# The fourth head of the last attention pass by token halves, and a half of x2 in another tile

## The reference, cut to what matters

```python
attn = softmax(einsum('bthd,bshd->bhts', q, k) * scale)          # 16 heads of 128
attn_out = einsum('bhts,bshd->bthd', attn, v) @ out_w + out_b
x = x + gate1 * attn_out
x2 = _ln(x) * (1.0 + scale2) + shift2
h = gelu(x2 @ ffn_w1 + ffn_b1)
x = x + gate2 * (h @ ffn_w2 + ffn_b2)
```

## Time and profile before

| what | before |
|---|---|
| median of 3 runs | 482.5 us (482.31 to 483.1) |
| the profiled execution: its time | 482.44 us |
| its span on the core | 480.6 us |
| TensorE's granted clock, mean | 0.999 |
| busy in the span: PE / DVE / ACT / POOL | 467.4 / 389.3 / 318.9 / 48.0 us |

### The profile page before, as it was taken

How to read it: one execution, slowest core, us unless ns; L and a number is a source line. 1 busy time by engine, 2 the same in 40 slices (tenths; PEclk the granted TensorE clock), 3 DMA queues, 4 the chain that set the end, 5 groups by cost and what they waited for, 6 DMA issues and landing times.

```text
span 480.6 us, 13808 instructions
## 1 busy us (share of the span) xinstructions
PE 467.4 (97%) x5271; PEld 334.8 (70%) x5271; DVE 389.3 (81%) x1368; ACT 318.9 (66%) x950; POOL 48.0 (10%) x78
## 2 busy tenths in 40 slices
PE   7999999999999999999899999999999999999997
PEld 4455776557656676568545444788898988989886
DVE  4969895779768899997896997888888888888884
ACT  1677964788477966887476965565665656656563
POOL 3010240223020320223000000000000000000000
PEclk9999999999999999999999999999999999999999
DMA  8992510100201000000000000000000000000000
GB/s 283 419 388 70 135 45 22 62 25 23 66 22 44 22 0 2 0 2 1 1 1 1 0 1 0 3 3 1 0 1 11 12 0 12 0 12 11 1 12 23
DMA packets 10399, 20.85 MB, mean 43 GB/s; under 512 B 1472, under 2 KB 4992, under 8 KB 9728
## 3 DMA queue, kind: packets, MB, share of 16 engines
q1 hardware_dynamic: 9808, 19.89, 12.0%
q10 hardware_dynamic: 560, 0.60, 0.4%
HBM read 19.40 MB, written 1.08 MB: 43 GB/s over the span
## 4 chain that ended last, share of the span: by engine, by line
PE 88%; DVE 4%; ACT 3%; DMA 1%; issue 1%; POOL 1%; SPq 0%; DVEq 0%
PE bank L884 58%; PE score L884 27%; PE spare L884 2%; DMA ao_sb<-xtok 1%; POOL ptx L507 1%; ACT ptx L632 1%; ACT ao_sb L585 1%; DVE drive L1459 1%; ACT x L532 0%; ACT th L810 0%; DVE drive L1463 0%; DVE q_group L2112 0%; DVE tok_stats L1406 0%; DVE acc L1551 0%; DVE drive L1614 0%
## 5 line engine op out<-in xcount | busy, mean ns | idle before, releaser
L884 PE MATMUL bank<-x,pairs_store 128*128 128x512 f16 x384 | 86.3, 379 | 0.5 <-ACT x L532 0.4
L884 PEld LDWEIGHTS bank<-x,pairs_store 128*128 128x128 f16 x384 | 36.9, 98 | 43.4 <-issue 1.4
L507 POOL TENSOR_TENSOR ptx<-pt,ptx 32x256 f16<-32x256 f32 x62 | 43.2, 697 | 176.2 <-ACT ptx L632 172.8
L884 PE MATMUL score<-cub,neg_eye 128*128 128x64 f32 x256 | 55.6, 299 | 0.0
L585 ACT ACTIVATE big<-bank,head_b 128x512 f16<-128x512 f32 x60 | 39.8, 685 | 17.4 <-PE bank L884 17.0
L2026 DVE TENSOR_TENSOR thlo<-th 128x64 f16<-128x64 f32 x128 | 28.8, 225 | 26.0 <-ACT th L811 24.8
L884 PE MATMUL score<-th,coup_part 128*128 128x32 f16 x1024 | 46.2, 177 | 0.9
L884 PE MATMUL bank<-pairs_store,ao_sb 128*128 128x256 f16 x360 | 43.0, 273 | 0.7 <-issue 0.2
L884 PE MATMUL bank<-pairs_store,x 128*128 128x512 f16 x192 | 43.4, 379 | 0.0
L810 ACT ACTIVATE th<-score 128x64 f16<-128x64 f32 x96 | 21.5, 224 | 31.7 <-PE score L884 28.9
L884 PEld LDWEIGHTS bank<-pairs_store,ao_sb 128*128 128x128 f16 x360 | 34.0, 98 | 7.5 <-DVE ao_sb L1652 1.5
(11 more groups left out here) (252 smaller groups left out, 1052.1 us busy)
## 6 DMA issues: line engine op xcount, KB each, us to landing
wqk_sb<-wqk SPq DMA_DIRECT2D x16, 256.0 KB, 2.7
wv_sb<-wv SPq DMA_DIRECT2D x4, 512.0 KB, 5.4
wo_sb<-wo SPq DMA_DIRECT2D x4, 512.0 KB, 4.2
f_sb<-ffn_w SPq DMA_DIRECT2D x2, 1024.0 KB, 14.7
ao_sb<-xtok SPq DMA_DIRECT2D x4, 256.0 KB, 5.8
x_sb<-xT SPq DMA_DIRECT2D x1, 1024.0 KB, 12.5
w_sb<-w1T SPq DMA_DIRECT2D x1, 1024.0 KB, 16.1
w_sb<-w2T SPq DMA_DIRECT2D x1, 1024.0 KB, 16.9
```

The lines of the kernel that those rows point to most:

```text
L507: nc.gpsimd.tensor_tensor(ptx[s, 1, :, s], pt[s], ptx[s, 0, :, s], ALU.subtract).then_inc(ptx_ready, 1)
L884: return nc.tensor.matmul(dst, lhsT, rhs, start=start, stop=stop, **kw)
```

## The change

In the last pass, the fourth head's work after the scores is cut into two token halves. DVE and ACT copy, shift, exponentiate, normalise and place half 0, then half 1, and `mix_half` forms the values' products of one half at a time. On PE, `out_project(0, 3, [0, 1])` and `mix_half(3, 1)` stand behind the output products of quarters 0 and 1, and those of quarters 2 and 3 for the last two heads stand behind `turn_normed(0)`, in the place of eight `unread` matmuls. `ada_late(SHIFT2)` moves forward into `spare`. On DVE, `low_last_pv([1])` stands between the layer norm's statistics and its root, and `take_heads(2)` and `take_heads(3)` stand one place later. ACT's `empty_x2(0)` follows `x1_high(NH)`. The modulated first half of x2 is written to `centred`, since `drive` still holds the gates of quarters 2 and 3. The first layer's blocks get the uses 163, 164, 162, 165, 166, 168, 169, 167 in the place of 162, 165, 166, 163, 164, 167, 168, 169. Lines that are only "..." mark what is left out.

```diff
...
-USE_F1 = [[AFTER + n for n in (2, 5, 6, 3, 4, 7, 8, 9)], [AFTER + 3 * KB + MB + m for m in range(MB)]]
+USE_F1 = [[AFTER + n for n in (3, 4, 2, 5, 6, 8, 9, 7)], [AFTER + 3 * KB + MB + m for m in range(MB)]]
...
+            if i == NQUAD - 1 and j == QUAD - 1:
+                for h in range(NH):
+                    gs = slice(h * G // 2, (h + 1) * G // 2)
+                    pool.wait_ge(full[bank_of(LAST_PV[j - 1] + h)], i * NPAR + count_of(LAST_PV[j - 1] + h))
+                    for q in range(NB4 // 2):
+                        s = slice(q * T, (q + 1) * T)
+                        pool.wait_ge(high_placed, i * (QUAD * NB4) + NB4 * (j + h) + q + 1)
+                        nc.gpsimd.tensor_tensor(ptx[s, 1, gs, s], pt[s, gs], ptx[s, 0, gs, s], ALU.subtract
+                                                ).then_inc(half_placed[h], 1)
+                return
             if j == QUAD - 1:
-                use = (LAST_PV if i == NQUAD - 1 else USE_PV)[j - 1] + 1
+                use = USE_PV[j - 1] + 1
...
-            for q in range(NB4 // 2 if i == NQUAD - 1 and j == QUAD - 1 else NB4):
+            for q in range(NB4):
...
-    pool.wait_ge(ptx_ready, NQUAD * QUAD * NB4)
+    for h in range(NH):
+        pool.wait_ge(half_placed[h], NB4)
...
-            nc.scalar.activation(x1_pair[:, 0, k, s], drive[:, k, s], ACT.Copy).then_inc(x1_high_ready, 1)
+            src = centred[:, k] if n == NH else drive[:, k, s]
+            nc.scalar.activation(x1_pair[:, 0, k, s], src, ACT.Copy).then_inc(x1_high_ready, 1)
...
+        def copy_half(h):
+            act.wait_ge(scores_ready, NQUAD * QUAD + h)
+            for q in range(NB4 // 2):
+                s, gs = slice(q * T, (q + 1) * T), slice(h * G // 2, (h + 1) * G // 2)
+                nc.scalar.activation(sraw[s, gs], s8[s, gs, s], ACT.Copy).then_inc(half_copied[h], 1)
...
+        def exps_half(h):
+            gs = slice(h * G // 2, (h + 1) * G // 2)
+            act.wait_ge(shifted, NQUAD * QUAD + h)
+            nc.scalar.activation(pe_[:, gs], sc[:, gs], ACT.Exp, scale=SCALE / WSCALE ** 2).then_inc(exp_ready, 1)
...
+        def place_high_half(h):
+            use = LAST_PV[QUAD - 2] + h
+            act.wait_ge(full[bank_of(use)], i * NPAR + count_of(use))
+            act.wait_ge(pt_ready, NQUAD * QUAD + h)
+            for q in range(NB4):
+                s, gs = slice(q * T, (q + 1) * T), slice(h * G // 2, (h + 1) * G // 2)
+                nc.scalar.activation(ptx[s, 0, gs, s], pt[s, gs], ACT.Copy).then_inc(high_placed, 1)
...
-        copy_scores(3, NB4 // 2 if last else NB4)
-        place_high(2)
-        exps(3)
-        if not last:
+        if last:
+            copy_half(0)
+            copy_half(1)
+            place_high(2)
+            exps_half(0)
+            exps_half(1)
+            place_high_half(0)
+            empty_pv(2)
+            empty_pv(3, [0])
+            place_high_half(1)
+            mlp_highs(5, 7)
+            empty_pv(3, [1])
+            mlp_highs(7, 8)
+        else:
+            copy_scores(3)
+            place_high(2)
+            exps(3)
...
-        empty_pv(2, [0])
-        place_high(3)
-        empty_pv(2, [1])
-        if last:
-            mlp_highs(5, 7)
-        else:
+            empty_pv(2, [0])
+            place_high(3)
+            empty_pv(2, [1])
...
-        empty_pv(3)
-        if last:
-            mlp_highs(7, 8)
-        else:
+            empty_pv(3)
...
+    act.wait_ge(first_heads_out, 1)
...
+    x1_high(NH)
+    act.wait_ge(last_full, 1)
...
-    x1_high(NH)
...
-                last = parts3(score[:, g // 4, (g % 4) * P:(g % 4 + 1) * P], q, k)
-            last.then_inc(scores_ready, 1)
+                done = parts3(score[:, g // 4, (g % 4) * P:(g % 4 + 1) * P], q, k)
+                if g == G - 1 or last and j == QUAD - 1 and g == G // 2 - 1:
+                    done.then_inc(scores_ready, 1)
...
+        def mix_half(j, h):
+            base = i * (QUAD * NB4) + NB4 * (j + 1)
+            late = j == QUAD - 1
+            pe.wait_ge(high_placed, base + NB4 * h if late else base)
+            dst = score[:, h] if late else fill(use_pv[j] + h)
+            for g in range(4 * h, 4 * h + 4):
+                at = dst[:, (g % 4) * P:(g % 4 + 1) * P]
+                for part in range(2):
+                    mm(at, v_sb[:, g, part, j * DH:(j + 1) * DH], ptx[:, 0, g], g % 4 == 0 and part == 0, False,
+                       skip_group_check=True)
+            if late:
+                pe.wait_ge(half_placed[h], NB4)
+            else:
+                pe.wait_ge(ptx_ready, base)
+            for g in range(4 * h, 4 * h + 4):
+                done = mm(dst[:, (g % 4) * P:(g % 4 + 1) * P], v_sb[:, g, 0, j * DH:(j + 1) * DH], ptx[:, 1, g],
+                          False, g % 4 == 3, skip_group_check=True)
+            if late:
+                done.then_inc(pv_full, 1)
+            else:
+                done.then_inc(full[bank_of(use_pv[j] + h)], 2)
...
                     if first:
-                        pe.wait_ge(ada2_ready, 4)
+                        pe.wait_ge(ada2_ready, 5)
...
+            elif last and (pair, c) == (0, 3):
+                done.then_inc(first_heads_out, 1)
...
+        if last:
+            mix_half(2, 0)
+            mix_half(2, 1)
+            out_project(0, 2, [0, 1])
+            mix_half(3, 0)
+            out_project(1, 0, [2])
+            out_project(1, 1, [2])
+            pe.wait_ge(ada2_ready, 4)
+            ada_late(SHIFT2, spare)
+            out_project(1, 0, [3])
+            out_project(1, 1, [3])
+            mix_half(3, 1)
+            out_project(0, 3, [0, 1])
+            return out_project
...
-    attention_pass(NQUAD - 1, True)
+    out_project = attention_pass(NQUAD - 1, True)
...
-    ada_late(SHIFT2, fill(USE_F1[0][3]))
-    unread(score[:, 0], 3)
+    pe.wait_ge(pv_taken, NQUAD * NH)
+    unread(score[:, 0], 4)
...
-    unread(fill(USE_F1[0][4])[:], 8)
+    for c in (2, 3):
+        out_project(1, c, [2, 3])
...
-    pe.wait_ge(ada2_ready, 5)
...
+    def modulated(h, k):
+        return drive[:, k, HALF:N] if h else centred[:, k]
...
-        s = slice(h * HALF, (h + 1) * HALF)
...
-        V.tensor_tensor(tok(drive[:, k, s]), tok(score[:, k]), mod(SCALE2, k, h), ALU.mult).then_inc(turned_read, 1)
+        V.tensor_tensor(tok(modulated(h, k)), tok(score[:, k]), mod(SCALE2, k, h), ALU.mult).then_inc(turned_read, 1)
...
-        s = slice(h * HALF, (h + 1) * HALF)
...
-        V.tensor_tensor(tok(drive[:, k, s]), tok(drive[:, k, s]), mod(SHIFT2, k, h), ALU.add).then_inc(normed, 1)
+        V.tensor_tensor(tok(modulated(h, k)), tok(modulated(h, k)), mod(SHIFT2, k, h), ALU.add).then_inc(normed, 1)
...
-        V.tensor_tensor(x1_pair[:, 1, k, s], drive[:, k, s], x1_pair[:, 0, k, s], ALU.subtract).then_inc(x1_low_ready, 1)
+        V.tensor_tensor(x1_pair[:, 1, k, s], modulated(h, k), x1_pair[:, 0, k, s], ALU.subtract).then_inc(x1_low_ready, 1)
...
+        def half_strips(h):
+            gs = halves_of(h)
+            dve.wait_ge(scores_ready, NQUAD * QUAD + h)
+            for q in range(NB4 // 2, NB4):
+                s = slice(q * T, (q + 1) * T)
+                V.tensor_copy(sraw[s, gs], s8[s, gs, s]).then_inc(half_copied[h], 1)
...
+        def shift_half(h):
+            gs = halves_of(h)
+            dve.wait_ge(half_copied[h], NB4)
+            own.step(V.tensor_reduce(smax[:, gs], sraw[:, gs], AX_X, ALU.max))
+            own.wait()
+            V.tensor_tensor(sc[:, gs], sraw[:, gs], smax[:, gs].unsqueeze(2).broadcast_to([P, G // 2, T]), ALU.subtract
+                            ).then_inc(shifted, 1)
...
+        def normalise_half(h):
+            gs = halves_of(h)
+            dve.wait_ge(exp_ready, NQUAD * QUAD + h)
+            own.step(V.tensor_reduce(ssum[:, gs], pe_[:, gs], AX_X, ALU.add))
+            own.wait()
+            own.step(V.reciprocal(srec[:, gs], ssum[:, gs]))
+            own.wait()
+            own.step(V.tensor_tensor(pn[:, gs], pe_[:, gs], srec[:, gs].unsqueeze(2).broadcast_to([P, G // 2, T]), ALU.mult))
+            own.wait()
+            dve.wait_ge(ptx_ready, (NQUAD * QUAD - 1) * NB4)
+            V.transpose(pt[:, gs].rearrange("p g t -> p (g t)"), pn[:, gs].rearrange("p g t -> p (g t)")
+                        ).then_inc(pt_ready, 1)
...
-        def place_last_low():
-            use = LAST_PV[QUAD - 2] + 1
+        def place_last_low(h):
+            use, gs = LAST_PV[QUAD - 2] + h, halves_of(h)
...
-            dve.wait_ge(high_placed, i * (QUAD * NB4) + QUAD * NB4)
+            dve.wait_ge(high_placed, (NQUAD * QUAD + h) * NB4)
...
-                V.tensor_tensor(ptx[s, 1, :, s], pt[s], ptx[s, 0, :, s], ALU.subtract).then_inc(ptx_ready, 1)
+                V.tensor_tensor(ptx[s, 1, gs, s], pt[s, gs], ptx[s, 0, gs, s], ALU.subtract).then_inc(half_placed[h], 1)
...
-            last_strips(3)
-            shift(3)
+            half_strips(0)
+            shift_half(0)
```

(29 more changed lines are left out.)

## The result

The changed kernel took 483.96 us, median of 7 runs (483.56 to 484.8), against 482.65 for the kernel before beside it: a ratio of 1.0031, 95% interval 1.0021 to 1.0042. It is slower by 1.3 us. The profiled execution took 483.65 (482.44 before), its span is 481.9 (480.6 before). PE is busy 466.1 us, DVE 390.2, ACT 320.3, POOL 48.5.

What follows compares the result with a forecast made beforehand. PE bounds the kernel (busy 467.4 of 480.6 us), so later starts of its first or second layer delay the end one for one. 0.45 + 0.1 + 0.4 + 1.24 = 2.2 us, from 482.44 to 484.6; range 483.0 to 486.2.

Steps and rivals of the forecast that it cites:

- Part 4: Before the second layer: PE must wait for the gelu of block 7, not block 6; plus 1.24 us.
- Part 3: In the first layer: the third block waits for take_heads(2) to free bank 3; plus 0.4 us (0 to 0.5).
- part 2: low_last_pv([1]) in the layer norm, mostly hidden by ACT's table load; plus 0.1 us (0 to 0.6).
- the signs named: Changed profile: take_heads(0) at 229.2 to 229.6, half subtractions 0.3 to 1.0 us, 1.2 us PE gap before second layer.
- part 1: Softmax by halves: DVE's added operations and holds by POOL start take_heads(0) 0.45 us later (-0.3 to +1.0).
- the walk: DVE's queue timed step by step from half_strips(0) at 218.26 to take_heads(0) at 229.4, for 228.96 before.
- C: DVE meets POOL in normalise_half and both placements too, layer norm a whole 0.6 later; near 4 us, 486.5; chance 0.09.
- A: Before the second layer: block 7's bank costs nothing, something else starts the layer; 1.0 us, 483.4; chance 0.10.
- B: DVE keeps up before take_heads(0), which starts 1.65 us earlier; about 482.5, or 481.3 with block 7's bank hidden; chance 0.13.
- D: TensorE's clock falls to 1.2 GHz between 233 and 237; first layer adds up to 9.24 us, 493.8; chance 0.02.

Runs made afterwards that it cites:

- e1_banks: The changed kernel with blocks 6 and 7 of the first layer exchanged between their banks: 482.65 us, 0.23 over the kernel before, ratio 1.0009.
- e4_pool: The changed kernel with five more POOL operations on two SBUF operands behind head 2's low parts: 484.9 us in one execution.
- e8_best_fill: The changed kernel with third block on bank 1, blocks 6 and 7 exchanged, ACT's copies interleaved, ada_late(SHIFT2) and its reader later, eight unread matmuls: 481.44 us, ratio 0.9977.
- e6_whole: The changed kernel with the fourth head's work undivided, as before, and both halves' low parts before take_heads(0): 484.26 us, ratio 1.0039.
- e5_best: e8_best_fill without its eight added matmuls: 481.30 us, ratio 0.9973.
- e2_third: The changed kernel with the first layer's third block on bank 1, fourth on bank 3, ACT's copies interleaved: 483.45 us, ratio 1.0025.

## Why the prediction was right

**The direction and the main terms of the loss.** 483.96 us stands in the range of 483.0 to 486.2 and 0.6 under the forecast of 484.6; slower was forecast with 0.80. Part 4 (+1.19 for +1.24) carries most of it, and e1_banks shows it by its one edit. It came from reading which instruction last held a bank, and from a chain in which the block before was already tied to the start of the second layer. Part 3 (+0.39 for +0.4) and part 2 (+0.07 for +0.1) came as worked out: ACT's layer norm started at 235.34 for 235.55, so of the 0.7 us of `low_last_pv([1])` only 0.06 got past ACT's table load. Of the signs named, the wait of PE for a DVE row before the third block (0.69) and the idle time released by the gelu (1.30) are there; `take_heads(0)` at 228.69 is outside 229.2 to 229.6, but not before the 228.5 that would have refuted the account; the first subtraction took 0.29 and so was not held, the second took 0.41 and was.

**The term that was mis-sized is part 1**, 0.7 us too high. The step that failed is "subtraction held to the end of POOL's second operation, about 220.0, done 220.15", and the one behind it, "subtraction held again, done 221.65". The subtractions ended at 219.49 and 220.90, with holds of 0 and 0.12 for the 0.7 and 0.25 that I had given them. The first started at 219.20, ahead of POOL's second operation at 219.24, and was not held at all. By the prediction's own figures this could be seen: POOL's operations stand 0.73 apart from 218.59, so its second starts at 219.32, and the reduction was to end at 219.18. The second subtraction came that much earlier and met the end of POOL's third operation, 220.76. So `normalise_half(0)` ended at 222.0 for 222.85, and PE's `out_project(0, 2)` started at 222.93 for 223.5. From there on the walk was right with an offset of 0.5 to 0.8 us: the reader of `ada_late(SHIFT2)` ran at 227.80, where I had `ada_late` itself end at 228.3, and `place_last_low(1)` ended at 228.66 for 229.4. The rule that I used, "each such DVE operation starts streaming only when the running POOL operation ends", held in all five rows of the table under e4_pool; what I got wrong is which operation was running.

**The bound of part 1 held, narrowly** (-0.27 in -0.3 to +1.0): with almost no hold the part came out at its lower bound, and the range held because the other three parts were right. Three slips of the arithmetic change no verdict: the ten pairs at 0.12 are 1.2 us and not 1.3; part 3 has a lower bound of 0 and enters the sum with 0.1; and the terms named for C, with part 3, add up to 4.4 and not to near 4.

**The rivals.** A is refuted by e1_banks. B named the right place but needed `low_pv(2, [0])` done by 224.3; it started at 224.66. e8_best_fill made `take_heads(0)` earlier by another way, without `ada_late` and its reader ahead of it, and brought 0.84 us where B named 1.65. C did not occur. D is true in part: its chance of 0.02 was too low. The mean clock is lower in a third of the executions, and in the two traces of such executions it falls to 1.2 GHz behind the wait for `low_last_pv([1])`, the place named. But that costs 1 us and not up to 9, since it is back before the first layer. My argument against it, that PE was busy 1.62 of the first 4 us at a clock of 1.00 and 3.43 of 4 here, took the row of the kernel before for a stretch in which the change removed PE's work. In the changed kernel PE was busy 2.15 of the 4 us from 230 to 234 (windows of its trace, where the clock did not fall), and the start of a kernel, where the clock stayed at 1.00 at less, was no stand-in for that. By the rule of the Trainium skill ("TensorE: Matmul & The Clock Gate", Part 1) that too little activity halves the array's clock, the runs agree with it.

**What stays open.** One execution of the changed kernel took 484.67 us at a clock of 0.999. Full clock does not mean equal times: e6_whole's profiled execution (484.87 at 1.0) starts `ada_late(SCALE2)` at 217.75 for 217.06, so it had lost 0.69 us before the stretch that is changed; whether 484.67 is of that kind is not known. Why e5_best with a gap of 1.08 us shows no fall in 11 executions, and the kernels with two such gaps do, was not separated further; at a share of a third, none in 11 would be chance about one time in 75.

## What to carry to other kernels

When buffers are renumbered, look which instruction is the last to hold each buffer that the next stage needs at once: a late one there cost a whole step of the engine that empties it (1.24 us), and exchanging two numbers gave it back. An instruction moved forward on one engine makes its reader wait on another; look what is queued behind that reader. When an operation is expected to be held by another engine's, write down which one is running when it starts; 0.04 us decided here who waited. And matmuls that nobody reads may be bought time: if a change opens gaps on PE, compare the granted clock of many executions, not only of one.

## What the runs showed of the hardware

TensorE's granted clock fell to 0.50 behind two gaps of 1.1 and 1.2 us with matmuls in between, in the two traces taken of such an execution (e2_third, e4_pool). The mean clock says that it fell in 15 of 44 executions of kernels of that order of work, in all five with gaps of 1.16 and 2.44 us (traced in one), and in two of 56 of the kernel before.

A DVE operation with two SBUF operands that starts while a POOL operation of the same kind is running ends 0.14 or 0.15 us behind it for 128 elements, and 0.29 for 256; unheld it takes 0.29 and 0.42. When DVE starts first, by 0.04 us, it is POOL's operation that is longer, 0.78 for 0.66.
